# Graph attention on one core: the softmax issued in front of the other tiles' work, the finished rows made by VectorE in one operation

## The chip, the cores and the metric

One core of a Trainium2 chip runs the whole kernel. The metric is the device time of one execution in microseconds (us). Engines: PE is TensorE's matmul, PEld its weight load, DVE VectorE, ACT ScalarE, POOL GpSimd, SP SyncE, which here only issues DMAs.

## The reference, cut to what matters

Two layers follow one another: a graph attention on x (4 x 1024 rows of 512 features), then a transformer block (projections, attention, output projection, MLP) on its result. The change lies in the first. For each row and each of two directions d (the adjacency and its transpose), 16 heads attend to the first 20 rows of the same example:

```python
self_feat = concat(v, q) @ W_self.T + b_self
output = self_feat
for d in range(2):
    A = adj_f if d == 0 else swapaxes(adj_f, 1, 2)       # 11 labels
    A = A[:, :, :20, :]
    cond, vb = A.sum(-1), A @ w_bias + b_bias
    aff = einsum(q_d, k_d) / sqrt(32)
    aff = where(cond > 0, aff, -9e15) + vb
    w = softmax(aff)                                     # over 20
    output = output + (w @ kv) @ Wout_d + bout_d
return v + relu(output)
```

## The kernel before, in words

The program runs stage after stage, each a block of five instruction streams that ends with a barrier of all engines: `graph_tables`, `graph_attention`, `projections`, `attention`, `output_projection`, `mlp`. `graph_tables` folds the weights into tables, so that in `graph_attention` a tile of 128 rows needs one product for all logits (640 columns: 16 heads, 2 directions, 20 keys), one for the features (512 columns) and a small one that adds the attention's values onto the features in the same PSUM bank. Products are done as three products of split float32 (a high and a rest part).

`graph_attention` walks over 32 tiles, k = 0 to 31. Every engine has its own order, written out by hand, with semaphores between them:

- **TensorE**, in iteration k: in k = 18, 20, 22 and 24 four transposes of the next stage's rows (`z_transposes`, L615); `logits(k)` (L636 into `a_pa`, waits for `xl_done` and `lg_done`); `transposes(k + 1)` of x (L626, L627); `weights(k - 1)`, six transposes of the softmax (L668, waits for `p_done`); `features(k)` (L636 into `a_po`, two banks; waits until the rows of tile k - 2 are made from that bank, L658); `values(k - 1)` (L676, waits for `wt_copied`).
- **VectorE**, in `softmax(k)`: adds the bias to the logits (L769, twice), max (L777), subtraction of the max (L778, `sub_done`); the rest part of the next x (`x_rest`, L718); a flag column (`flag(k + 2)`, L713); `bias(k + 1)`: sum of the weighted adjacency (L725, waits for ScalarE's `prod_done`), count of labels (L726), mask (L727), their sum (L728); in k = 9, 11, ..., 23 the rest of an eighth of the next stage's weights (L790); in k = 10 to 24 the next stage's first rows (`first_rows`, L733 to L760); then, after Exp, the sum (L793), reciprocal (L794) and product (L795, `p_done`).
- **ScalarE**: rounds x out of PSUM (`x_rounded(k + 1)`, L541, L542), copies the transposed softmax (`weights_out(k - 1)`, L548 to L550), makes the row sum of x (`row_sum(k + 2)`, L560) and the eleven weighted adjacency planes (`weighted(k + 1)`, L569), then Exp (L599), then Relu of the rows (`rows_out(k - 1)`, L556), and on even k from 8 to 22 rounds an eighth of the next stage's weights (L605).
- **GpSimd** adds x to the rows after Relu (L524), frees the x buffer (`x_free`), and issues the store of y (L527); once, at k = 14, it makes the rstd of the first rows.
- **SP** loads x (four buffers, L490, waits for `x_free`) and the adjacency (two buffers, L492, waits for `adj_used`), at k = 5, 13 and 21 the next example's tables, at k = 6 the 4 MB of the next stage's weights (L504), at k = 8 the first four tiles of y.

The function `link` raises a semaphore when an operation is done and lets VectorE wait for it, so that the next operation reads finished data.

Of the kernel before, what the change touches and what calls it, by code (L numbers as in the profile page):

```python
# [14 lines left out]
ALU = mybir.AluOpType  # L15
# [377 lines left out]
def graph_attention(nc, t, ident, mod_t, gp, cg, pn, y, wqk, wqk_raw, x_first):  # L393
# [15 lines left out]
    with ExitStack() as ctx:  # L409
        def sb(name, shape, dt=F32):  # L410
# [26 lines left out]
        px = banks(ctx, nc, "a_px", 2)  # L437
        pw = banks(ctx, nc, "a_pw", 2)
        (st_in, ws_done, zeros_set, dve_step, rs_done, xt_done, xh_copied, xl_done, o_done, a_done, adj_used, lg_done,
         sub_done, exp_done, p_done, wt_done, wt_copied, pv_done, relu_done, y_done, x_free, w_in) = sems(  # L440
            ctx, nc, "graph", "st_in ws_done zeros_set dve_step rs_done xt_done xh_copied xl_done o_done a_done adj_used lg_done sub_done "
            "exp_done p_done wt_done wt_copied pv_done relu_done y_done x_free w_in", first=True)
        x_in = sems(ctx, nc, "graph", " ".join("x_in%d" % i for i in range(4)))
        wqk_in, wqk_rounded = sems(ctx, nc, "graph", "wqk_in wqk_rounded")
        (rows_in, half_set, stats_done, aggr_done, var_ready, rstd_ready, z_done, zt_done, xm_done, first_rounded, first_split) = sems(
# [6 lines left out]
        def x5s(k):  # L452
            return x5[k % 4]
# [55 lines left out]
        @block.gpsimd  # L509
        def _(pool):  # L510
            for k in range(2):
                pool.memset(c4[k][:].bitcast(F32), 0.0).then_inc(zeros_set, 1)
                pool.memset(bd[k][:], 0.0).then_inc(zeros_set, 1)
            for k in range(4):
                pool.memset(x5[k][:, F:], 0.0).then_inc(zeros_set, 1)
            pool.wait_ge(zeros_set, 8)
            for k in range(4):
                pool.memset(x5[k][:, F + 1:F + 4:2], 1.0).then_inc(zeros_set, 1)

            pool.memset(half[:], -0.5).then_inc(half_set, 1)  # L520
            pool.sem_inc(x_free, 4)
            for k in range(B * BT):
                pool.wait_ge(relu_done, k + 1)
                pool.tensor_tensor(yo[k % 2][:], yo[k % 2][:], x5s(k)[:, 0:F], ALU.add).then_inc(y_done, 1)  # L524
                pool.wait_ge(y_done, k + 1)
                pool.sem_inc(x_free, 1)
                pool.dma_start(y[k * P:(k + 1) * P, :], yo[k % 2][:]).then_inc(y_out[k % 2], 16)  # L527
                if k == LN0 + GT:
                    pool.wait_ge(half_set, 1)
                    pool.wait_ge(var_ready, 1)  # L530
                    pool.tensor_tensor(rstd[:], ve[:], half[:], ALU.pow).then_inc(rstd_ready, 1)
            for n in range(2):
                pool.wait_ge(y_out[n], 16 * B * BT // 2)

        @block.scalar
        def _(act):
            def x_rounded(k):
                act.wait_ge(xt_done, k + 1)
                if k >= 2:
                    act.wait_ge(o_done, k - 1)  # L540
                act.copy(xh[k % 2][:, 0:F], px[0][:])  # L541
                act.copy(xh[k % 2][:, F:], px[1][:, 0:P]).then_inc(xh_copied, 1)  # L542

            def weights_out(k):
                act.wait_ge(wt_done, k + 1)
                if k:
                    act.wait_ge(pv_done, k)
                act.copy(wt[:, 0:4, :], pw[0][0:HC * HJ, :].rearrange("p (c n) -> p c n", n=P))  # L548
                act.copy(wt[:, 4, :], pw[1][0:HC * HJ, 0:P])
                act.copy(wt[0:HJ, 5, :], pw[1][0:HJ, P:2 * P]).then_inc(wt_copied, 1)  # L550

            def rows_out(k):
                act.wait_ge(pv_done, k + 1)
                if k >= 2:
                    act.wait_ge(y_out[k % 2], 16 * (k // 2))
                act.activation(yo[k % 2][:], po[k % 2][:], ACT.Relu).then_inc(relu_done, 1)  # L556

            def row_sum(k):
                act.wait_ge(x_in[k % 4], 16 * (k // 4 + 1))
                act.activation(x_copy[:], x5s(k)[:, 0:F], ACT.Copy, accum_out=rs[:, k % 2:k % 2 + 1]).then_inc(sum_done, 1)  # L560

            def weighted(k):
                act.wait_ge(adj_in[k % 2], 16 * (k // 2 + 1))
                if k == 0:
                    act.wait_ge(w_in, 32)
                else:
                    act.wait_ge(prod_read, k)
                for l in range(L0):
                    i = act.activation(prod[:, l, :], adj[k % 2][:, l, :], ACT.Copy, scale=wrow[:, l:l + 1])  # L569
                i.then_inc(prod_done, 1)  # L570

            def modulate(n):
                act.wait_ge(zt_done, n + 1)
                if n:
                    act.wait_ge(first_split, n)
                for c in range(KC):
                    i = act.activation(xm[:, c, :], px[0][:, c * P:(c + 1) * P], ACT.Identity,
                                       bias=mod_t[:, 0, c:c + 1], scale=mod_t[:, 0, KC + c:KC + c + 1])
                i.then_inc(xm_done, 1)

            n = B * BT
            tables(act, 0)
            row_sum(0)
            x_rounded(0)
            row_sum(1)
            weighted(0)
            for k in range(n):
                if (k - Z0) % 2 == 0 and 0 < (k - Z0) // 2 <= GT:
                    modulate((k - Z0) // 2 - 1)
                if k + 1 < n:  # L590
                    x_rounded(k + 1)
                if k:
                    weights_out(k - 1)
                if k + 2 < n:
                    row_sum(k + 2)
                if k + 1 < n:
                    weighted(k + 1)
                act.wait_ge(sub_done, k + 1)
                act.activation(lg[k % 2][:], lg[k % 2][:], ACT.Exp).then_inc(exp_done, 1)  # L599
                if k:  # L600
                    rows_out(k - 1)
                w = (k - W0) // 2
                if (k - W0) % 2 == 0 and 0 <= w < len(WN):
                    act.wait_ge(wqk_in, 16)
                    act.copy(w_part(wqk[0], w), w_part(wqk_raw, w)).then_inc(wqk_rounded, 1)  # L605
            weights_out(n - 1)
            rows_out(n - 1)

        @block.tensor
        def _(pe):  # L610
# [43 lines left out]
            def features(k):  # L654
                if k == 0:
                    pe.wait_ge(ws_done, 2)
                if k >= 2:
                    pe.wait_ge(relu_done, k - 1)  # L658
                product(po[k % 2][:], (xh[k % 2], xl[k % 2]), (wsh, wsl), c4[(k // BT) % 2][:, 0:F]).then_inc(o_done, 1)

            def weights(k):
# [35 lines left out]
        def _(dve):  # L697
            steps = [0]

            def link(ins):  # L700

                steps[0] += 1
                ins.then_inc(dve_step, 1)
                dve.wait_ge(dve_step, steps[0])
# [4 lines left out]
            def flag(k):  # L709
                if k == 0:  # L710
# [2 lines left out]
                dve.tensor_scalar(x5s(k)[:, F:F + 3:2], rs[:, k % 2:k % 2 + 1].to_broadcast([P, 2]), 0.0, None,  # L713
                                  ALU.not_equal).then_inc(rs_done, 1)

            def x_rest(k):
                dve.wait_ge(xh_copied, k + 1)
                dve.tensor_tensor(xl[k % 2][:], px[0][:], xh[k % 2][:, 0:F], ALU.subtract).then_inc(xl_done, 1)  # L718

            def bias(k):  # L720

                s = sm[k % 2]
                dve.wait_ge(adj_in[k % 2], 16 * (k // 2 + 1))
                dve.wait_ge(prod_done, k + 1)
                dve.reduce_sum(s[:, 0, :], prod[:].rearrange("p l j -> p j l"), axis=AX.X).then_inc(prod_read, 1)  # L725
                link(dve.reduce_sum(s[:, 1, :], adj[k % 2][:].rearrange("p l j -> p j l"), axis=AX.X))  # L726
                link(dve.tensor_scalar(s[:, 2, :], s[:, 1, :], 0.0, NEG, ALU.is_le, ALU.mult))  # L727
                i = dve.scalar_tensor_tensor(out=s[:, 3, :], in0=s[:, 0, :], scalar=wrow[:, L0:L0 + 1], in1=s[:, 2, :],  # L728
                                             op0=ALU.add, op1=ALU.add)
                link(i)  # L730
                dve.sem_inc(adj_used, 1)
# [30 lines left out]
            def softmax(k):  # L762
# [17 lines left out]

                if k + 1 < B * BT:
                    x_rest(k + 1)
                if k + 2 < B * BT:
                    flag(k + 2)
                if k + 1 < B * BT:
                    bias(k + 1)
                w = (k - 1 - W0) // 2
                if (k - 1 - W0) % 2 == 0 and 0 <= w < len(WN):
                    dve.wait_ge(wqk_rounded, w + 1)
                    dve.tensor_tensor(w_part(wqk[1], w), w_part(wqk_raw, w), w_part(wqk[0], w), ALU.subtract)  # L790
                first_rows(k)
                dve.wait_ge(exp_done, k + 1)
                link(dve.reduce_sum(dn[:], z[:], axis=AX.X))  # L793
                link(dve.reciprocal(dn[:], dn[:]))  # L794
                dve.tensor_tensor(z[:], z[:], dn[:].unsqueeze(2).to_broadcast([P, 2 * H0, M0]),  # L795
                                  ALU.mult).then_inc(p_done, 1)

            n = B * BT
            flag(0)
# [1137 lines left out]
```

## Time and profile before

| | us |
|---|---|
| median of 3 runs | 3224.87 (3224.06 to 3225.6) |
| the profiled execution, its own time | 3222.87 |
| its span | 3221.1 |
| `graph_attention`, first transpose of x to last store's issue | 184.4 to 536.4 |

| engine | busy us | share of the span |
|---|---|---|
| PE | 3076.9 | 96% |
| PEld | 2440.8 | 76% |
| DVE | 1850.5 | 57% |
| ACT | 1341.9 | 42% |
| POOL | 845.7 | 26% |

Busy shares are means over stages with different limits. A row of the timeline gives the start of an instruction from the span's start, its duration, engine, line, operation, what it writes and reads with partitions and elements, how many were merged (x), and in brackets the idle time of its engine before it and what ended that.

### The profile page before, as it was taken

What the parts mean: (1) busy time and instruction counts of PE and PEld (TensorE: products, weight loads), DVE (VectorE), ACT (ScalarE), POOL (GpSimd) and SP (SyncE); (2) the same over time, 40 slices, a digit from 0 to 9 for tenths busy, and PEclk for the clock granted to TensorE, in tenths of its full rate; (3) what the DMA queues carried; (4) which work ended last, traced back from release to release, by engine and by line L of the source; (5) the groups of instructions that cost most, each with busy time, mean ns of one, the idle gap of its engine ahead of it and who ended that gap; (6) DMA issues with size and microseconds to landing.
All of it is one profiled execution on the core that took longest, in us unless ns stands there. A gap on an engine that the chain in (4) does not pass through costs nothing. (4 is left out here: it accounts for less than half of the span.)

```text
span 3221.1 us, 62151 instructions
## 1 busy us (share of the span) xinstructions
PE 3076.9 (96%) x24696; PEld 2440.8 (76%) x24696; DVE 1850.5 (57%) x2743; ACT 1341.9 (42%) x2786; POOL 845.7 (26%) x571
## 2 busy tenths in 40 slices
PE   8969998999999799999999999999896999999999
PEld 5968887888888577777777777777685888888887
DVE  4357785212211388888888888888564334333432
ACT  2145653222222277777777777777002111111111
POOL 1011112100000143444444344436454111111110
PEclk9989998999999899999999999999997999999999
DMA  4554222333332333233333333332563001010100
GB/s 140 178 183 145 96 70 97 107 106 104 104 114 102 105 110 96 80 94 92 94 80 93 92 94 81 92 97 70 215 241 111 1 27 33 26 33 26 33 14 14
DMA packets 196342, 297.28 MB, mean 92 GB/s; under 512 B 27889, under 2 KB 105713, under 8 KB 194055
## 3 DMA queue, kind: packets, MB, share of 16 engines
q1 hardware_dynamic: 182528, 276.54, 27.6%
q0 software_dynamic: 4288, 14.68, 1.3%
q10 hardware_dynamic: 9296, 2.77, 0.4%
q8 instruction: 172, 2.82, 0.4%
q14 instruction: 58, 0.47, 0.0%
HBM read 190.44 MB, written 103.49 MB: 91 GB/s over the span
## 5 line engine op out<-in xcount | busy, mean ns | idle before, releaser
L1338 DVE TENSOR_REDUCE b_nm<-b_ps 128x1 f32<-128x1024 f32 x512 | 601.6, 1216 | 16.3 <-PE b_ps L1279 3.2
L1245 ACT ACTIVATE b_p<-b_ps,b_nm 128x1024 f32<-128x1024 f32 x512 | 565.0, 1113 | 40.8 <-DVE b_nm L1338 40.8
L1308 PE MATMUL b_po<-b_pt,b_v 128*64 128x256 f32 x4096 | 498.3, 385 | 0.8 <-DVE b_pt L1358 0.8
L1250 ACT ACTIVATE b_pt<-b_tp_act 128x512 f32<-128x512 f32 x512 | 308.6, 603 | 305.1 <-PE b_tp_dve L1291 305.1
L1358 DVE COPY b_pt<-b_tp_dve 128x512 f32<-128x512 f32 x512 | 351.2, 686 | 117.3 <-PE b_tp_dve L1291 117.2
L1291 PEld LDWEIGHTS b_tp_act<-ident,b_p 64*128 64x128 f32 x4096 | 312.2, 138 | 128.8 <-issue 100.6
L1308 PEld LDWEIGHTS b_po<-b_pt,b_v 128*64 128x64 f32 x4096 | 271.9, 136 | 128.6 <-ACT b_pt L1250 0.9
L1291 PE MATMUL b_tp_act<-ident,b_p 64*128 64x64 f32 x4096 | 347.8, 225 | 2.4 <-issue 2.4
L1291 PE MATMUL b_tp_dve<-ident,b_p 64*128 64x64 f32 x4096 | 347.7, 225 | 0.0
L1700 ACT ACTIVATE d_ge<-d_pf,d_b 128x512 f32<-128x512 f32 x128 | 88.2, 689 | 596.6 <-PE d_pf L1722 596.6
L1291 PEld LDWEIGHTS b_tp_dve<-ident,b_p 64*128 64x128 f32 x4096 | 311.8, 138 | 2.4
L1789 DVE CAST d_gh<-d_ge 128x512 fp32r<-128x512 f32 x128 | 69.7, 544 | 417.8 <-ACT d_ge L1700 417.7
L1279 PE MATMUL b_ps<-b_kl,b_qh 64*128 64x512 f32 x1024 | 225.9, 435 | 18.4 <-DVE b_kl L1382 14.5
L1191 POOL TENSOR_TENSOR b_qh<-b_raw_q,b_ones 128x1024 fp32r<-128x1024 f32 x62 | 117.5, 1895 | 426.2 <-DMA b_raw_k<-k_t 400.7
L955 ACT ACTIVATE p_qk<-p_pm 128x512 f32<-128x512 f32 x128 | 76.6, 598 | 322.6 <-PE p_pm L977 322.6
L1733 PE MATMUL d_po<-d_w2h,d_gl 128*128 128x512 f32 x512 | 205.4, 401 | 2.0 <-DVE d_gl L1791 2.0
L1279 PE MATMUL b_ps<-b_kh,b_qh 64*128 64x512 f32 x1024 | 205.7, 393 | 0.0
L1279 PE MATMUL b_ps<-b_kh,b_ql 64*128 64x512 f32 x1024 | 204.4, 391 | 0.0
L1733 PE MATMUL d_po<-d_w2h,d_gh 128*128 128x512 f32 x512 | 202.5, 395 | 0.0
L1733 PE MATMUL d_po<-d_w_rest,d_gh 128*128 128x512 f32 x512 | 201.9, 394 | 0.0
L1660 POOL TENSOR_TENSOR d_y<-d_y,d_gated 128x512 f32<-128x512 f32 x32 | 43.2, 1374 | 559.7 <-DVE d_gated L1796 559.7
L1195 POOL TENSOR_TENSOR b_ql<-b_raw_q,b_qh 128x1024 fp32r<-128x1024 f32 x62 | 147.6, 2380 | 4.9
(253 smaller groups left out, 5666.8 us busy)
## 6 DMA issues: line engine op xcount, KB each, us to landing
b_raw_q<-q_t SPq DMA_DIRECT2D x128, 256.0 KB, 4.3
q_t<-p_qk SPq DMA_DIRECT2D x64, 256.0 KB, 2.0
k_t<-p_qk SPq DMA_DIRECT2D x64, 256.0 KB, 2.0
v_n<-p_vs SPq DMA_DIRECT2D x32, 512.0 KB, 3.2
b_raw_k<-k_t SPq DMA_DIRECT2D x128, 128.0 KB, 4.2
b_v<-v_n SPq DMA_DIRECT2D x32, 512.0 KB, 3.9
b_rb<-inv SPq DMA_DIRECT2D x64, 256.0 KB, 3.8
o_t<-b_ot SPq DMA_DIRECT2D x32, 512.0 KB, 2.6
```

What stands on the lines that cost most here:

```text
L955: act.activation(qk[n % 4][:], pm[n % 4][:], ACT.Copy, scale=float(D1) ** -0.5 if n < PAIRS else 1.0).then_inc(qk_done, 1)
L1191: pool.tensor_tensor(qh[u][h][:], raw_q[h][:], one, ALU.mult)
L1195: pool.tensor_tensor(ql[u][h][:], raw_q[h][:], qh[u][h][:], ALU.subtract)
L1245: act.activation(pr[k % 4][:], ps[k % 2][:], ACT.Exp, bias=nm[:, k % 4:k % 4 + 1], accum_out=rs[:, n:n + 1]).then_inc(exp_done, 1)
L1250: act.activation(dst, src, ACT.Copy).then_inc(t_out[0], 1)
L1279: mm = pe.matmul(ps[k % 2][:, half * SK:(half + 1) * SK], q[u][h][HALF[half], q0:q0 + P], key[u][h][HALF[half], :], start=(n == 0), stop=( ...
L1291: mm = pe.transpose(tp(j, k)[:, kc * D1:(kc + 1) * D1], pr[k % 4][HALF[j], kc * P:(kc + 1) * P], ident[HALF[j], HALF[j]])
L1308: mm = pe.matmul(po[rows, (blk % 2) * 2 * P:(blk % 2 + 1) * 2 * P], vt[u][:, kc, rows], pt[blk % 2][h][:, kc, :], start=(kc == 0), stop=(k ...
L1338: dve.tensor_reduce(nm[:, k % 4:k % 4 + 1], ps[k % 2][:], axis=AX.X, op=ALU.max, negate=True).then_inc(max_done, 1)
L1358: dve.tensor_copy(dst, src).then_inc(t_out[1], 1)
L1700: act.activation(ge[j % 2][:], pf[j % 2][:], ACT.Gelu, bias=b1[:, j:j + 1]).then_inc(gelu_done, 1)
L1733: mm = pe.matmul(po[n][:], a[j % 2][:, cols], w[:, j, :], start=(j == 0 and m == 0), stop=(j == NH - 1 and m == 2))
```

## The change

VectorE's softmax waits for Exp and does its sum, reciprocal and product right behind `x_rest(k + 1)`, in front of `flag(k + 2)`, `bias(k + 1)`, the next stage's weights and the first rows; ScalarE does Exp right behind `weights_out(k - 1)`, in front of the row sum and the weighted adjacency. In `bias`, the label count and the mask come in front of the wait for the weighted adjacency. The finished rows, max(rows, 0) + x, are made by one `scalar_tensor_tensor` of VectorE out of PSUM, behind `bias(k + 1)`; ScalarE's Relu and GpSimd's addition are gone, and the semaphore `relu_done` with them. GpSimd still frees the x buffer and issues the store.

```diff
@@ semaphores
-         sub_done, exp_done, p_done, wt_done, wt_copied, pv_done, relu_done, y_done, x_free, w_in) = sems(
+         sub_done, exp_done, p_done, wt_done, wt_copied, pv_done, y_done, x_free, w_in) = sems(
@@ gpsimd
             for k in range(B * BT):
-                pool.wait_ge(relu_done, k + 1)
-                pool.tensor_tensor(yo[k % 2][:], yo[k % 2][:], x5s(k)[:, 0:F], ALU.add).then_inc(y_done, 1)
                 pool.wait_ge(y_done, k + 1)
                 pool.sem_inc(x_free, 1)
@@ scalar
-            def rows_out(k):
-                act.wait_ge(pv_done, k + 1)
-                if k >= 2:
-                    act.wait_ge(y_out[k % 2], 16 * (k // 2))
-                act.activation(yo[k % 2][:], po[k % 2][:], ACT.Relu).then_inc(relu_done, 1)
...
                 if k:
                     weights_out(k - 1)
+                act.wait_ge(sub_done, k + 1)
+                act.activation(lg[k % 2][:], lg[k % 2][:], ACT.Exp).then_inc(exp_done, 1)
                 if k + 2 < n:
                     row_sum(k + 2)
                 if k + 1 < n:
                     weighted(k + 1)
-                act.wait_ge(sub_done, k + 1)
-                act.activation(lg[k % 2][:], lg[k % 2][:], ACT.Exp).then_inc(exp_done, 1)
-                if k:
-                    rows_out(k - 1)
...
             weights_out(n - 1)
-            rows_out(n - 1)
@@ tensor, features(k)
                 if k >= 2:
-                    pe.wait_ge(relu_done, k - 1)
+                    pe.wait_ge(y_done, k - 1)
@@ vector
+            def rows_out(k):
+                dve.wait_ge(pv_done, k + 1)
+                if k >= 2:
+                    dve.wait_ge(y_out[k % 2], 16 * (k // 2))
+                dve.scalar_tensor_tensor(out=yo[k % 2][:], in0=po[k % 2][:], scalar=0.0, in1=x5s(k)[:, 0:F],
+                                         op0=ALU.max, op1=ALU.add).then_inc(y_done, 1)
@@ vector, bias(k)
                 dve.wait_ge(adj_in[k % 2], 16 * (k // 2 + 1))
+                link(dve.reduce_sum(s[:, 1, :], adj[k % 2][:].rearrange("p l j -> p j l"), axis=AX.X))
+                dve.tensor_scalar(s[:, 2, :], s[:, 1, :], 0.0, NEG, ALU.is_le, ALU.mult)
                 dve.wait_ge(prod_done, k + 1)
-                dve.reduce_sum(s[:, 0, :], prod[:].rearrange("p l j -> p j l"), axis=AX.X).then_inc(prod_read, 1)
-                link(dve.reduce_sum(s[:, 1, :], adj[k % 2][:].rearrange("p l j -> p j l"), axis=AX.X))
-                link(dve.tensor_scalar(s[:, 2, :], s[:, 1, :], 0.0, NEG, ALU.is_le, ALU.mult))
+                link(dve.reduce_sum(s[:, 0, :], prod[:].rearrange("p l j -> p j l"), axis=AX.X))
+                dve.sem_inc(prod_read, 1)
@@ vector, softmax(k)
                 if k + 1 < B * BT:
                     x_rest(k + 1)
+                dve.wait_ge(exp_done, k + 1)
+                link(dve.reduce_sum(dn[:], z[:], axis=AX.X))
+                link(dve.reciprocal(dn[:], dn[:]))
+                dve.tensor_tensor(z[:], z[:], dn[:].unsqueeze(2).to_broadcast([P, 2 * H0, M0]),
+                                  ALU.mult).then_inc(p_done, 1)
                 if k + 2 < B * BT:
                     flag(k + 2)
                 if k + 1 < B * BT:
                     bias(k + 1)
+                if k:
+                    rows_out(k - 1)
...
                 first_rows(k)
-                dve.wait_ge(exp_done, k + 1)
-                link(dve.reduce_sum(dn[:], z[:], axis=AX.X))
-                link(dve.reciprocal(dn[:], dn[:]))
-                dve.tensor_tensor(z[:], z[:], dn[:].unsqueeze(2).to_broadcast([P, 2 * H0, M0]),
-                                  ALU.mult).then_inc(p_done, 1)
+                if k == B * BT - 1:
+                    rows_out(k)
```

## Rows read from the trace of the kernel before

**Rows 1.** Waits of TensorE's weight loads, 180 to 545 us: total, times, longest
```profile
PEld a_pw L668 <- DVE a_lg L795: 30.6, 32, 2.5
```

**Rows 2.** Timeline of a plain tile: TensorE and its weight loads around the logits' end
```profile
493.52 0.31 PE L636 MATMUL a_pa<-a_c,a_xh 128*128 128x320 f32 x1
...
494.44 0.59 PEld L668 LDWEIGHTS a_pw<-ident,a_lg 128*120 128x120 f32 x6 [0.30 <-DVE a_lg L795]
...
495.04 0.76 PEld L636 LDWEIGHTS a_po<-a_wsh,a_xh 128*128 128x128 f32 x4
```

**Rows 3.** Timeline of GpSimd: the additions of tiles 0, 26 and 30
```profile
210.96 1.29 POOL L524 TENSOR_TENSOR a_yo<-a_yo,a_x 128x512 f32<-128x512 f32 x1 [34.67 <-ACT a_yo L556]
...
490.54 1.29 POOL L524 TENSOR_TENSOR a_yo<-a_yo,a_x 128x512 f32<-128x512 f32 x1 [7.51 <-ACT a_yo L556]
...
530.35 1.25 POOL L524 TENSOR_TENSOR a_yo<-a_yo,a_x 128x512 f32<-128x512 f32 x1 [7.52 <-ACT a_yo L556]
```

**Rows 4.** Timeline of VectorE in the same plain tile
```profile
490.34 1.00 DVE L726 TENSOR_REDUCE a_sm<-a_adj 128x40 f32<-128x440 int32 x1
491.37 0.51 DVE L727 TENSOR_SCALAR a_sm<-a_sm 128x40 f32<-128x40 f32 x1
491.91 0.26 DVE L728 SCALAR_TENSOR_TENSOR a_sm<-a_sm,a_wrow 128x40 f32<-128x40 f32 x1
492.32 0.82 DVE L793 TENSOR_REDUCE a_dn<-a_lg 128x32 f32<-128x640 f32 x1
493.17 0.35 DVE L794 RECIPROCAL a_dn<-a_dn 128x32 f32<-128x32 f32 x1
493.56 0.82 DVE L795 TENSOR_TENSOR a_lg<-a_lg,a_dn 128x640 f32<-128x640 f32 x1
494.30 0.88 DVE L769 TENSOR_TENSOR a_lg<-a_pa,a_sm 128x320 f32<-128x320 f32 x2
495.33 0.82 DVE L777 TENSOR_REDUCE a_mx<-a_lg 128x32 f32<-128x640 f32 x1
496.18 0.83 DVE L778 TENSOR_TENSOR a_lg<-a_lg,a_mx 128x640 f32<-128x640 f32 x1
496.92 0.68 DVE L718 TENSOR_TENSOR a_xl<-a_px,a_xh 128x512 fp32r<-128x512 f32 x1
497.52 0.16 DVE L713 TENSOR_SCALAR a_x<-a_rs 128x2 f32<-128x2 f32 x1
499.38 1.00 DVE L725 TENSOR_REDUCE a_sm<-a_prod 128x40 f32<-128x440 f32 x1 [1.70 <-ACT a_prod L569]
```

**Rows 5.** Timeline of ScalarE in the same plain tile
```profile
496.14 0.64 ACT L560 ACTIVATE a_x_copy<-a_x 128x512 f32<-128x512 f32 x1
...
496.77 2.51 ACT L569 ACTIVATE a_prod<-a_adj,a_wrow 128x40 f32<-128x40 int32 x11
...
499.18 0.73 ACT L599 ACTIVATE a_lg<-a_lg 128x640 f32<-128x640 f32 x1
```

**Rows 6.** VectorE's groups, 208 to 520 us: count, busy us, mean ns, idle
```profile
L790 DVE TENSOR_TENSOR w_qk_rest<-w_qk_raw,w_qk_high 128x1024 fp32r<-128x1024 f32 x8 | 9.8, 1225 | 1.2
```

**Rows 7.** Timeline of ScalarE: the row sum that waited for its load of x
```profile
248.99 0.63 ACT L560 ACTIVATE a_x_copy<-a_x 128x512 f32<-128x512 f32 x1 [2.09 <-DMA a_x<-x]
```

**Rows 8.** Timeline of VectorE in the first tile, GpSimd idle
```profile
191.59 0.18 DVE L727 TENSOR_SCALAR a_sm<-a_sm 128x40 f32<-128x40 f32 x1
```

**Rows 9.** Timeline of TensorE's weight loads: one of the four z-transposes
```profile
424.84 0.42 PEld L615 LDWEIGHTS a_px<-ident,a_zn 128*128 128x128 f32 x4
```

**Rows 10.** Timeline of SP's queue in the plain tile
```profile
491.91 0.33 SPq L490 DMA_DIRECT2D a_x<-x  x1
```

**Rows 11.** Tile a_x, 180 to 540 us: the loads' time from issue to landing
```profile
DMA to landing us min/median/max: 2.6/2.7/6.4
```

**Rows 12.** Timeline of the stage's end: the last Relu and the last store's issue
```profile
533.82 0.60 ACT L556 ACTIVATE a_yo<-a_po 128x512 f32<-128x512 f32 x1 [2.23 <-PE a_po L676]
...
536.35 0.56 POOL L527 DMA_DIRECT2D y<-a_yo  x1 [0.59 <-POOL a_yo L524]
```

More of the change, by code:

```diff
@@ L439, in graph_attention @@
         (st_in, ws_done, zeros_set, dve_step, rs_done, xt_done, xh_copied, xl_done, o_done, a_done, adj_used, lg_done,
-         sub_done, exp_done, p_done, wt_done, wt_copied, pv_done, relu_done, y_done, x_free, w_in) = sems(
+         sub_done, exp_done, p_done, wt_done, wt_copied, pv_done, y_done, x_free, w_in) = sems(
             ctx, nc, "graph", "st_in ws_done zeros_set dve_step rs_done xt_done xh_copied xl_done o_done a_done adj_used lg_done sub_done "
-            "exp_done p_done wt_done wt_copied pv_done relu_done y_done x_free w_in", first=True)
+            "exp_done p_done wt_done wt_copied pv_done y_done x_free w_in", first=True)
         x_in = sems(ctx, nc, "graph", " ".join("x_in%d" % i for i in range(4)))
```

## The prediction

> **What bounds the kernel now.** The change stays inside the graph-attention stage, so I read the waits of that stage first. The row to see is TensorE's wait for the normalised softmax: the weight load of the transposes that turn the softmax (L668) waited for VectorE's last multiplication (L795) in each of the 32 tiles, 30.6 us in all [rows 1]; no other wait of TensorE comes back tile by tile. Then the timeline of one plain tile, with the end of its logits, 493.52 + 0.31 = 493.83, as zero. TensorE goes on with the transposes of the next tile, stops 0.30 us before L668, starts the features at 1.21 [rows 2], and is dense from there to the next logits. The last four turns are plain, (530.35 - 490.54) / 4 = 9.95 us by GpSimd's additions [rows 3], so a plain turn holds 9.65 us of TensorE's own work. The 30 turns between the first and the last full tile took 530.35 - 210.96 = 319.4 us, 10.65 each [rows 3]: 20.9 us above 30 plain turns.
>
> What makes the turn is a loop over three engines: VectorE's L795, TensorE's transposes L668, ScalarE's copies out of them, row sum and eleven weighted copies (L569), and back to VectorE, which idles 1.70 us for L569 at L725, then does the bias and only then the softmax's sum, reciprocal and product [rows 4, 5]. Everything else VectorE does behind the bias lengthens this loop in full: the eight rests of the next stage's weights at 1.23 us each (L790 [rows 6]) and the next stage's first rows. That is the 20.9, but for some 2.6 around one late load of x (ScalarE idled 2.09 us for it [rows 7]), which leaves 18.3 us in tiles 9 to 24.
>
> **The change, part by part.**
>
> *Softmax in front.* After the change the product of tile k hangs on logits(k) alone, through the adds, max, subtraction, Exp, sum, reciprocal and product. Start to start [rows 4, 5]: 1.03 + 0.85, then subtraction, Exp and two semaphore hops 0.83 + 0.73 + 0.10 = 1.66 (the rest of the next x, 0.68, fits inside), then 0.85 + 0.39 + 0.74: done 5.5 us after zero. TensorE wants it in front of the next L668, at 9.65 + 0.31 = 9.96. The 4.4 us between them are the cover; the 30.6 us go, all but the last tile's 0.3, which has nothing behind it: **-30.3 us**. ScalarE must reach Exp in time: the rounding of x and the three copies occupy it until about 2.3, the subtraction ends at 2.8. The row sum and weighted copies, 0.63 + 2.51 [rows 5], now follow Exp and end at 6.7; VectorE wants them at 6.9, so its 1.70 us of idleness goes too. The adjacency count is put ahead of that wait, and adds nothing; it is the cover of L569.
>
> *Finished rows on VectorE.* ScalarE loses 32 Relus, GpSimd 32 additions of 1.29 us [rows 3], neither on the path except at the end. VectorE gains 32 operations of 128x512 with one source in PSUM. No row shows this operation at this size. The nearest is L718, 128x512 out of PSUM with a second source in SBUF: 0.68 us, next start 0.60 later [rows 4]. That is the lower end and what I take. The upper end is one column at half that rate: L790 did 1024 columns in 1.23 us [rows 6], so 1.23. The same operation at 40 columns (L728) took 0.26 against 0.18 for L727 undisturbed [rows 4, 8], which does not exclude it. The Trainium skill speaks against the change here ("Vector Engine (DVE) Microarchitecture Reference", "7. Points that are easy to get wrong"): this operation halves its throughput when both sources are non-bf16 and in SBUF. One source here is in PSUM, so its condition is not met as written; no row decides it. By it the sum would be that of the first rival below.
>
> *GpSimd off VectorE's back.* L727 took 0.51 us while GpSimd's addition ran (490.54 to 491.83) and ended as that did; at 191.59, with GpSimd idle, 0.18 [rows 3, 4, 8]. The addition goes, so I count 0.18.
>
> *VectorE's new turn.* 1.03 + 0.85 + 1.66 + 0.85 + 0.39 + 0.74, flag 0.15, adjacency count 1.03, mask 0.18, sum of the weighted copies 1.00 with 0.15 for its semaphore and wait, L728 0.41, rows 0.60: **9.05 us**, against TensorE's 9.65. A plain tile is TensorE's, with 0.6 us to spare. That cover is gone in tiles 9 to 24: the 18.3 us of extra work less 16 x 0.6, less the four z-transposes of 0.42 by which TensorE's turn is longer there [rows 9], leaves 7.0 us of backlog. What is late next are the rows: features(k+1) overwrite the bank of tile k-1 and wait until its rows are made. These end at 9.2 after zero, features want them at 9.65 + 0.91 = 10.56, so 1.35 us of backlog are free. The rest is paid: **+5.6 us**.
>
> *The queues.* The rows' operation now gives x's buffer free, 9.2 after zero or 0.45 before the next, where GpSimd's addition did it at 491.83, 2.0 before [rows 3]. SP issues the load 0.08 us later [rows 10], which behind GpSimd's wake-up is at -0.3; it lands after 2.7 [rows 11], at 2.4, and ScalarE wants it at 3.5. In the stretch of the 4 MB load, x landed after 6.4 us [rows 11]. Then the loop rows, load, row sum, weighted copies, sum, L728, rows is 0.3 + 6.4 + 0.63 + 2.51 + 0.1 + 1.15 + 0.41 + 0.70 = 12.2 against 9.65; less the 1.35 free: **+1.2 us**. Before, that event's 2.1 us sat in the 30.6. GpSimd's queue keeps its store and only loses the addition; the store's buffer was filled two turns ago. VectorE's wait for the values of tile k-1 (done at about 6) stands in front of the rows (8.5), with nothing idle.
>
> *The end of the stage.* From Relu's start 533.82 to the last store's issue 536.35 were 2.53 us [rows 12]; now one operation 0.70 and the same 0.6 to the issue: **-1.2 us**. It is exposed, since the next stage loads y behind a barrier.
>
> Sum: -30.3 + 5.6 + 1.2 - 1.2 = -24.7 on the profiled 3222.87 us (span 3221.1), 3198.2. The median of the runs shown lies 2.0 us higher, so **3200 us**. No later stage changes.
>
> **Rivals.**
>
> *The rows' operation at half rate.* VectorE's turn becomes 9.6, the plain spare 0.05: backlog 18.3 - 0.8 - 1.7 - 1.35 = 14.5, and the load's 2.5 are never made good: 3222.9 - 31.5 + 14.5 + 2.5 + 2.0 = 3210. For it: two float32 sources and L728's 0.26. Against it: L718. Chance 0.12.
>
> *VectorE is quicker than its gaps say.* The semaphore gaps between linked operations, some 0.4 us, could vanish in work in flight. At 8.6 the spare is 16 x 1.05 = 16.8 beside the 1.7, and the 18.3 fit in; only the load's 1.2 is left: 3222.9 - 31.5 + 1.2 + 2.0 = 3194.6. For it: a few 0.15 us gaps in the row starts. Against: they were there before. Chance 0.10.
>
> *Exp comes late.* If ScalarE reaches Exp not at 2.3 but a microsecond behind the subtraction (the copies wait for L668, which waits behind the transposes), VectorE idles in each tile, its turn is 10.05, with the extra work 10.65 on average: 3224, no change. This is also how the change fails to do what it says, the wait for L795 being replaced by one for Exp. Against it: the 0.5 us margin. Chance 0.05.
>
> *The x load closes a loop (slower).* At SP's queue: the loop above is 5.8 us plus the landing. At 2.7 it is 8.5; it takes over from TensorE at 3.85, equals the old 10.65 at 4.85, and at 5.2 every turn is 11.0, over 30 turns +10 us: 3235. Before, the buffer came free 1.5 us earlier against the same zero. For it: 6.4 was seen once. Against it: the median 2.7. Chance 0.05.
>
> **How the numbers follow.** My forecast has 0.68, the rivals 0.12, 0.10, 0.05, 0.05. A measurement of this kernel tells about 0.2%, 6.4 us, from no change. The first three cases lie below 3218: faster 0.90, same 0.05, slower 0.05. The range takes in the quick and the half-rate case, 3193 to 3211; the last two are left out.
>
> **What would show it.** Right: the wait of L668 near zero; a plain turn of 9.65 at the ends of the stage; in tiles 13 to 24 a wait of the features (L636) for VectorE's rows, about 6 us in all; rows at 0.7 us; L727 at 0.18; no wait of VectorE for L569; last store issued about 27 us earlier than 536. Wrong: rows of 1.2 us, a wait of the sum for Exp over 0.2 us a tile, or ScalarE waiting for x in plain tiles.

## The result: 3201.3 us, 0.74% faster

| | median us | runs | ratio to the kernel before, 95% interval |
|---|---|---|---|
| before | 3224.86 | 3224.06 to 3225.60 | |
| changed | 3201.26 | 3199.87 to 3203.45 | 0.9926 (0.9914 to 0.9939) |

The forecast was 3200, with 3193 to 3211 as its range. The profiled execution of the changed kernel is its slowest, 3203.45 us, so its trace shows more waiting than a typical run; `changed_again` below is a second trace of the same kernel. In the changed kernel's lines L766 is the adds, L774 the max, L775 the subtraction, L714 the rest of x, L781 to L783 sum, reciprocal and product, L702 the flag, L720 and L721 count and mask, L723 the sum of the weighted copies, L725 the last bias operation, L709 the finished rows, L657 the softmax's transposes, L625 the products.

The page of the changed kernel, its first two lines:

```profile
span 3201.7 us, 62119 instructions
PE 3076.4 (96%) x24696; PEld 2442.9 (76%) x24696; DVE 1861.2 (58%) x2775; ACT 1326.0 (41%) x2754; POOL 803.6 (25%) x539
```

TensorE's busy time is what it was (3076.9). VectorE gained 11 us, ScalarE lost 16, GpSimd 42; the span lost 19.4. A busy share says nothing of this: what went was TensorE's waiting. The waits of TensorE's weight loads in the stage, 180 to 545 us (total, times, longest):

```profile
PEld a_po L625 <- DVE a_yo L709: 7.2, 10, 2.4
PEld a_po L665 <- ACT a_wt L548: 1.3, 1, 1.3
PEld a_px L615 <- ACT a_xm L569: 1.1, 3, 0.4
PEld a_pw L657 <- DVE a_lg L783: 0.7, 1, 0.7
```

The wait for the softmax's product, 30.6 us in 32 tiles [rows 1], is one of 0.7 us in the last tile. What came in its place stands above it: the features wait for the finished rows in 10 tiles, 7.2 us. The weight loads of the features that waited, from the timeline:

```profile
255.82 0.76 PEld L625 LDWEIGHTS a_po<-a_wsh,a_xh 128*128 128x128 f32 x4 [2.36 <-DVE a_yo L709]
285.73 0.77 PEld L625 LDWEIGHTS a_po<-a_wsh,a_xh 128*128 128x128 f32 x4 [0.83 <-DVE a_yo L709]
325.19 0.76 PEld L625 LDWEIGHTS a_po<-a_wsh,a_xh 128*128 128x128 f32 x4 [0.71 <-DVE a_yo L709]
...
457.10 0.76 PEld L625 LDWEIGHTS a_po<-a_wsh,a_xh 128*128 128x128 f32 x4 [0.34 <-DVE a_yo L709]
```

The first, 2.4 us, is the late load of x. The other nine, 4.9 us, lie between 285 and 457 us. VectorE's other work (the weights' rests, the next stage's first rows) begins only at 294.5, so the wait at 285.73 is not backlog. It follows a second late load of x: one issued at 274.53 held ScalarE until 280.19, 5.7 us later, and VectorE idled for ScalarE's copies:

```profile
280.19 0.63 ACT L552 ACTIVATE a_x_copy<-a_x 128x512 f32<-128x512 f32 x1 [2.34 <-DMA a_x<-x]
```

```profile
283.35 1.00 DVE L723 TENSOR_REDUCE a_sm<-a_prod 128x40 f32<-128x440 f32 x1 [1.12 <-ACT a_prod L561]
```

Up to 380 us ScalarE waited for x four times more, 1.7 us in all. In the second trace it waits for no x after 250 us, and the features wait 2.3 us there instead of 4.9. So in this trace backlog and late loads are mixed; what delayed these later loads is open.

VectorE's timeline in a tile at the end of that stretch and the start of the next:

```profile
465.88 0.88 DVE L766 TENSOR_TENSOR a_lg<-a_pa,a_sm 128x320 f32<-128x320 f32 x2
466.91 0.82 DVE L774 TENSOR_REDUCE a_mx<-a_lg 128x32 f32<-128x640 f32 x1
467.76 0.83 DVE L775 TENSOR_TENSOR a_lg<-a_lg,a_mx 128x640 f32<-128x640 f32 x1
468.51 0.69 DVE L714 TENSOR_TENSOR a_xl<-a_px,a_xh 128x512 fp32r<-128x512 f32 x1
...
469.40 0.82 DVE L781 TENSOR_REDUCE a_dn<-a_lg 128x32 f32<-128x640 f32 x1 [0.20 <-ACT a_lg L587]
470.25 0.35 DVE L782 RECIPROCAL a_dn<-a_dn 128x32 f32<-128x32 f32 x1
470.64 0.83 DVE L783 TENSOR_TENSOR a_lg<-a_lg,a_dn 128x640 f32<-128x640 f32 x1
471.38 0.16 DVE L702 TENSOR_SCALAR a_x<-a_rs 128x2 f32<-128x2 f32 x1
471.45 0.99 DVE L720 TENSOR_REDUCE a_sm<-a_adj 128x40 f32<-128x440 int32 x1
472.48 0.18 DVE L721 TENSOR_SCALAR a_sm<-a_sm 128x40 f32<-128x40 f32 x1
472.58 0.99 DVE L723 TENSOR_REDUCE a_sm<-a_prod 128x40 f32<-128x440 f32 x1
473.72 0.26 DVE L725 SCALAR_TENSOR_TENSOR a_sm<-a_sm,a_wrow 128x40 f32<-128x40 f32 x1
474.21 0.69 DVE L709 SCALAR_TENSOR_TENSOR a_yo<-a_po,a_x 128x512 f32<-128x512 f32 x1 [0.23 <-DVE a_sm L725]
...
475.55 0.89 DVE L766 TENSOR_TENSOR a_lg<-a_pa,a_sm 128x320 f32<-128x320 f32 x2 [0.65 <-PE a_pa L625]
```

The product starts 4.8 us behind the adds. From 465.88 to 475.55 the turn is 9.67, TensorE's, and VectorE idles the last 0.65 of it. While it still catches up its turn is its own, to be read off SP's issues of x, which follow the rows: 466.05 to 474.98 is 8.93, then 474.98 to 484.63 is 9.65.

```profile
466.05 0.33 SPq L490 DMA_DIRECT2D a_x<-x  x1
...
474.98 0.33 SPq L490 DMA_DIRECT2D a_x<-x  x1
...
484.63 0.33 SPq L490 DMA_DIRECT2D a_x<-x  x1
```

The stage's end, last rows and last store, from VectorE's and GpSimd's timelines:

```profile
513.80 0.69 DVE L709 SCALAR_TENSOR_TENSOR a_yo<-a_po,a_x 128x512 f32<-128x512 f32 x1 [3.04 <-PE a_po L665]
...
515.09 0.54 POOL L525 DMA_DIRECT2D y<-a_yo  x1 [3.19 <-DVE a_yo L709]
```

The last store is issued 21.3 us earlier than the 536.35 of before [rows 12], and 1.29 us behind the start of the last rows instead of 2.53.

### The profile page after: what moved, and what is told of

Its sections match the earlier page's. It is cut to its first block and busy times, and to the rows that moved or that the text cites. A ratio compares the mean times of both kernels' runs of the same rounds, so it can differ in the third digit from the quotient of the medians.

```text
span 3201.7 us, 62119 instructions
## 1 busy us (share of the span) xinstructions
PE 3076.4 (96%) x24696; PEld 2442.9 (76%) x24696; DVE 1861.2 (58%) x2775; ACT 1326.0 (41%) x2754; POOL 803.6 (25%) x539
## 5 line engine op out<-in xcount | busy, mean ns | idle before, releaser
L1280 PE MATMUL b_ps<-b_kl,b_qh 64*128 64x512 f32 x1024 | 226.1, 436 | 18.3 <-DVE b_kl L1383 14.7
```

The costliest lines, as they stand in the source:

```text
L1280: mm = pe.matmul(ps[k % 2][:, half * SK:(half + 1) * SK], q[u][h][HALF[half], q0:q0 + P], key[u][h][HALF[half], :], start=(n == 0), stop=( ...
```

## The experiments

The ratios are to the kernel before as it was measured beside each version, 3224.1 to 3224.4 us. The diffs show the main places of each edit.

The theory going in: the softmax in front brings the whole gain; the rows on VectorE give some of it back, as backlog where VectorE has other work; TensorE's turn of 9.67 us is the floor. The rivals differ by experiment and stand in the expectations.

**The softmax alone.** The kernel before with only the softmax's and the bias' new order.

```diff
@@ gpsimd, against the changed kernel
+                pool.wait_ge(relu_done, k + 1)
+                pool.tensor_tensor(yo[k % 2][:], yo[k % 2][:], x5s(k)[:, 0:F], ALU.add).then_inc(y_done, 1)
...
@@ scalar, against the changed kernel
                 if k + 1 < n:
                     weighted(k + 1)
+                if k:
+                    rows_out(k - 1)
@@ vector, against the changed kernel
                     bias(k + 1)
-                if k:
-                    rows_out(k - 1)
```

> Only the softmax is moved to the front (with the bias' new order); Relu stays on ScalarE, the addition on GpSimd. Theory (the softmax in front brings all of the gain, and VectorE's added row operation gives some of it back as backlog in tiles 9 to 24): TensorE's wait for L795 falls from 30.6 us to under 1; VectorE's turn is some 0.5 us shorter than with the rows (8.4 against 8.9), so the 7.2 us that the features wait for rows in the changed kernel fall to about 0.5, and the stage's end costs 1.2 us more: about 3196 us, 29 below the kernel before. Rival (the rows on VectorE bring a part of the gain of their own, by freeing ScalarE and GpSimd): 3205 to 3215 us.

Measured: 3195.77 us (3194.57 to 3196.29), ratio to the kernel before 0.9911 (0.9896 to 0.9926). The waits of TensorE's weight loads:

```profile
PEld a_pw L668 <- DVE a_lg L787: 0.7, 1, 0.7
PEld a_pa L636 <- DVE a_xl L718: 0.6, 2, 0.3
```

No wait for rows is among them, and the theory's 3196 is met. So half of the change is faster than the whole, by 5.5 us of 3201.3. The late load of x is here too (issued at 241.20, ScalarE waits 3.39 us for it until 249.19), but TensorE loses only one of these 0.3 us to it: with the rows off VectorE a late x is nearly free.

**The rows alone.** The kernel before with only the rows moved.

```diff
                 if k + 1 < B * BT:
                     bias(k + 1)
+                if k:
+                    rows_out(k - 1)          # VectorE, scalar_tensor_tensor out of PSUM
...
                 first_rows(k)
                 dve.wait_ge(exp_done, k + 1)
```

> Only the rows are moved to VectorE; the softmax's second half stays behind the other work. Theory (the loop VectorE, TensorE, ScalarE, VectorE sets the turn, and the rows lie in it): each turn grows by the rows' 0.8 us less the 0.3 us that L727 no longer loses to GpSimd, 32 x 0.5 = 16, less 1.2 at the stage's end: about 3240 us. Rival (either half brings part of the gain): 3210 to 3220 us.

Measured: 3239.88 us (3237.27 to 3241.08), ratio 1.0047 (1.0033 to 1.0061): slower than before, as the theory had it. The old wait grew from 30.6 us, because the rows lie in the loop that leads to the product:

```profile
PEld a_pw L663 <- DVE a_lg L799: 40.0, 30, 3.9
```

That the time came out at the expected 3240 is partly luck. A plain turn is 10.28 us (L663 at 495.54 and 505.82), 0.33 more than before and not the 0.5 that the theory counts. The stage is 14.6 us longer, and the waits explain only 9.4 of them. Most of the rest is TensorE's granted clock. Three times it is at 0.50, the level of 1.2 GHz: from 260.0 to 263.0, from 349.0 to 352.0 and from 407.0 to 410.0 us, each time shortly behind a wait of TensorE (3.9, 2.3 and 2.2 us). Its mean is 0.89 over 255 to 270, 0.91 over 340 to 360 and 0.89 over 400 to 416, which is 1.6, 1.8 and 1.8 us of full clock, 5.2 together. The first of these stretches, with its granted clock behind the engines' busy times:

```profile
255.00:270.00 15.00, 11.36 (x64) 10.02 (x63) 11.97 (x22) 5.32 (x19) 1.08 (x2) 0.89 0.42 127
```

The kernel before never leaves 1.00 between 200 and 500 us, although its longest wait there is 2.5 us; and a wait of 2.4 us at 325.82 of this run was followed by no fall. What decides is not shown.

The parts don't add: -28.4 and +15.7 make -12.7 where both together make -23.6. Behind the softmax the rows lie in VectorE's spare time; in front of it they lie on the path.

**The bias' old order.** The changed kernel, with the adjacency count behind the wait for ScalarE's weighted copies again.

```diff
-                link(dve.reduce_sum(s[:, 1, :], ...adj...))
-                dve.tensor_scalar(s[:, 2, :], ...)
                 dve.wait_ge(prod_done, k + 1)
-                link(dve.reduce_sum(s[:, 0, :], ...prod...))
-                dve.sem_inc(prod_read, 1)
+                dve.reduce_sum(s[:, 0, :], ...prod...).then_inc(prod_read, 1)
+                link(dve.reduce_sum(s[:, 1, :], ...adj...))
+                link(dve.tensor_scalar(s[:, 2, :], ...))
```

> The changed kernel with the bias' own order as it was: the sum of the weighted copies first, then count and mask. Theory (the adjacency count is the cover of ScalarE's weighted copies): VectorE idles 1.0 us a tile for L569's copies, its turn goes from 8.93 to 9.9 us, so it and not TensorE sets the turn of 9.9 in plain tiles, and the 18.3 us of other work in tiles 9 to 24 are paid in full: about 3217 us. Rival (VectorE's spare 0.7 us takes it up, only the tiles 9 to 24 lose): 3205 us.

Measured: 3225.06 us (3222.10 to 3228.56), ratio 1.0003 (0.9994 to 1.0012): the whole gain is gone. Its waits, and VectorE's idle time for the copies in a plain tile:

```profile
DVE a_sm L721 <- ACT a_prod L561: 37.6, 32, 2.3
PEld a_po L625 <- DVE a_yo L709: 27.6, 27, 3.1
```

```profile
494.14 1.00 DVE L721 TENSOR_REDUCE a_sm<-a_prod 128x40 f32<-128x440 f32 x1 [0.95 <-ACT a_prod L561]
```

The mechanism is the theory's (0.95 us idle a tile where 1.0 was expected), the sum was not: 3217. VectorE's turn here is 9.85 us (x issued at 487.70, 497.56, 507.40), 0.10 less than the old plain turn, and on it come the same 18.3 us of other work and a late load, as before the change. That is the old time less a few us, and I had taken off some 8 too many. Of these 8, 1.6 are the granted clock: 0.50 from 261.5 to 264.0 us, behind a wait of 3.1 us for rows, a mean of 0.89 over 255 to 270. So the order of two small operations carries as much as the order of the softmax, once the rows lie on VectorE. This run does not say what it is worth without them.

**The rows at double cost.** The changed kernel with a second such operation in tiles 0 to 30, into a scratch tile; the output is unchanged.

```diff
+                if k < B * BT - 1:
+                    dve.scalar_tensor_tensor(out=extra[:], in0=po[k % 2][:], scalar=0.0, in1=x5s(k)[:, 0:F], ...)
                 dve.scalar_tensor_tensor(out=yo[k % 2][:], in0=po[k % 2][:], ...).then_inc(y_done, 1)
```

> The changed kernel with the rows' operation preceded in tiles 0 to 30 by a copy of itself into a scratch tile (no effect on the output): the price that a halved rate would have had. Theory (VectorE has 0.7 us to spare in a plain turn and none in tiles 9 to 24): the plain turn stays 9.67 us, 0.6 us in each of tiles 9 to 24 is paid in full and the free margin falls from 1.35 to 0.75: +9 to +10 us, about 3211 us. Rival (TensorE is the bound all through and the rows are hidden): within 2 us of the changed kernel.

Measured: 3215.09 us (3213.46 to 3216.30), ratio 0.9971 (0.9960 to 0.9982): 13.8 us above the changed kernel, not 9 to 10. The waits, and two of the features' loads ahead of the busy stretch:

```profile
PEld a_po L626 <- DVE a_yo L713: 18.9, 20, 2.9
```

```profile
223.56 0.77 PEld L626 LDWEIGHTS a_po<-a_wsh,a_xh 128*128 128x128 f32 x4 [0.64 <-DVE a_yo L713]
...
244.32 0.76 PEld L626 LDWEIGHTS a_po<-a_wsh,a_xh 128*128 128x128 f32 x4 [1.43 <-DVE a_yo L713]
```

VectorE's turn is 9.54 (its adds at 497.32 and 506.86). With 0.13 to spare it hardly works off what delays it, so TensorE waits in the first tiles already and enters the busy stretch with no free margin. The waits shown, 0.64 and 1.43 us, come 6 us behind the moments at which ScalarE had waited for x (217.50, 1.13 us; 238.18, 1.75 us): late loads again. Between the traces, the waits for rows grew by 11.7 us and those for the rest of x by 0.5; the granted clock, 0.50 from 258.0 to 261.0 us behind a wait of 2.9 us (mean 0.91 over 250 to 268), adds 1.6. The rival (rows hidden) is out; the theory's mechanism holds, with the first tiles and the clock left out of its sum.

**Both sources in SBUF.** One more operation of this kind in tiles 26 to 29, output unchanged.

```diff
+                if 26 <= k < 30:
+                    dve.scalar_tensor_tensor(out=extra[:], in0=stage[:, 0, :], scalar=0.0, in1=x5s(k)[:, 0:F], ...)
```

> The changed kernel with one more operation of the rows' kind in tiles 26 to 29, both float32 sources in SBUF, into a scratch tile (no effect on the output). If two float32 sources in SBUF halve the throughput, it takes 1.2 us; if the rate is that of the rows out of PSUM (0.69 us), 0.7. At 0.7 the plain turn stays 9.67 us in these tiles; at 1.2 the four tiles together run up 4 x 0.5 us of backlog, within the margin of 1.35 but for about 0.6 us.

Measured: 3199.78 us, one run. The operation by its tile (min, median, max ns), beside the rows of the changed kernel:

```profile
L711 DVE SCALAR_TENSOR_TENSOR a_extra<-a_stage,a_x x4: 691/692/693, 471.0 to 499.9; 128x512 f32<-128x512 f32 x4
```

```profile
L709 DVE SCALAR_TENSOR_TENSOR a_yo<-a_po,a_x x32: 685/692/693, 213.2 to 513.8; 128x512 f32<-128x512 f32 x32
```

0.69 us either way, no more than the subtraction of the same size (L714, 0.68). The rule cited in the prediction (the Trainium skill, "Vector Engine (DVE) Microarchitecture Reference", "7. Points that are easy to get wrong": half throughput with two non-bf16 sources in SBUF) is not what the chip does in this form of the operation, with float32 and without an accumulator; the measurement decides.

**The weights' rests on GpSimd.** The changed kernel; eight subtractions of 128x1024 leave VectorE's busy stretch.

```diff
                 pool.dma_start(y[k * P:(k + 1) * P, :], yo[k % 2][:]).then_inc(y_out[k % 2], 16)
+                w = (k - W0) // 2
+                if (k - W0) % 2 == 0 and 0 <= w < len(WN):
+                    pool.wait_ge(wqk_rounded, w + 1)
+                    pool.tensor_tensor(w_part(wqk[1], w), w_part(wqk_raw, w), w_part(wqk[0], w), ALU.subtract)
```

> The changed kernel, with the eight rests of the next stage's weights (9.7 us of VectorE in tiles 9 to 23) made by GpSimd, which has nothing else to do then. Theory (VectorE's backlog is what the features wait for): the 4.8 us of waits for rows in tiles 9 to 24 go, the 2.4 us at the late load of x stay: about 3196.5 us, 5 below the changed kernel. Rival (GpSimd's operation of some 2.4 us holds up VectorE's operations with two SBUF sources by what it spares them): 3201 us.

Measured: 3202.50 us (3201.59 to 3204.94), ratio 0.9934 (0.9921 to 0.9948): no gain, the rival's case. VectorE's group of the subtraction in the changed kernel, then in this one (count, busy us, mean ns, idle):

```profile
L775 DVE TENSOR_TENSOR a_lg<-a_lg,a_mx 128x640 f32<-128x640 f32 x30 | 24.8, 826 | 1.0
```

```profile
L779 DVE TENSOR_TENSOR a_lg<-a_lg,a_mx 128x640 f32<-128x640 f32 x30 | 35.9, 1195 | 1.0
```

11.1 us more in eight tiles, 1.39 each, where 1.22 each was taken off. The timeline of one:

```profile
293.15 2.41 POOL L529 TENSOR_TENSOR w_qk_rest<-w_qk_raw,w_qk_high 128x1024 fp32r<-128x1024 f32 x1
...
293.71 0.82 DVE L778 TENSOR_REDUCE a_mx<-a_lg 128x32 f32<-128x640 f32 x1
294.56 1.69 DVE L779 TENSOR_TENSOR a_lg<-a_lg,a_mx 128x640 f32<-128x640 f32 x1
```

The subtraction, both sources in SBUF, takes 1.69 us here instead of 0.83, up to 2.47 in other tiles, and Exp waits for it. In all eight it ends 0.7 us behind the end of GpSimd's operation (here 296.25 against 295.56), whenever it began: it makes little or no headway beside it. The max just before it, with one source, ran beside GpSimd at its usual 0.82. The rest of x begins only when GpSimd is done, so its 0.68 says nothing on this. The Trainium skill ("SBUF — State Buffer", "Who interferes with whom") has a two-source operation in SBUF contend with GpSimd's reads; the trace agrees.

**The load in four.** The changed kernel, the 4 MB of the next stage's weights in four loads.

```diff
-                    if k == W0 - 2:
-                        sp.dma_start(wqk_raw[:], ...[:, :, 0:2 * INNER]).then_inc(wqk_in, 16)
+                    if W0 - 2 <= k < W0 - 2 + KC:
+                        c = k - W0 + 2
+                        sp.dma_start(wqk_raw[:, c, :], ...[:, c, 0:2 * INNER]).then_inc(wqk_in, 16)
```

> The changed kernel, with the 4 MB load of the next stage's weights issued as four loads of 1 MB in four successive tiles. Theory (that load is what makes one x land after 8 us, and this costs 2.4 us of features' waits): the longest landing of x falls under 5 us, the 2.4 us go, the 4.8 us of backlog stay: about 3199 us. Rival (the late x comes from the tables' loads just before, or the cost only moves to other tiles): 3201 us, a landing of x still over 6 us.

Measured: 3197.04 us (3196.44 to 3197.70), ratio 0.9915 (0.9902 to 0.9929): 4.2 us below the changed kernel (3.5 below `changed_again`, whose runs lie above all of these), more than the 2.4 expected. The features' waits, and ScalarE's longest wait for x in the changed kernel and here:

```profile
PEld a_po L626 <- DVE a_yo L710: 2.6, 6, 0.7
```

```profile
250.32 0.63 ACT L552 ACTIVATE a_x_copy<-a_x 128x512 f32<-128x512 f32 x1 [3.92 <-DMA a_x<-x]
```

```profile
239.85 0.63 ACT L553 ACTIVATE a_x_copy<-a_x 128x512 f32<-128x512 f32 x1 [2.21 <-DMA a_x<-x]
```

The load of x behind the 4 MB landed after 8.0 us. Those issued among the four loads (245.40, 254.32, 264.00) landed after 2.7, 4.1 and 2.7. The wait shown last is for one issued just ahead of the first of the four, behind the tables' loads:

```profile
233.88 0.36 SPq L490 DMA_DIRECT2D a_x<-x  x1
```

It held ScalarE until 239.85, 6.0 us, so "under 5 us" was missed, and the tables' loads, which the rival names, may have their part. The longest landing that the profile lists, 5.0 us, is of a load at 331.97 that has nothing to do with the four; in the two traces of the changed kernel the same load took 5.2.

The features' waits fell from 7.2 to 2.6 us: from 2.4 to 0.7 at the late load, from 3.4 to 0.5 between 260 and 400 us, where this trace has no late x, and not behind 400 (1.5 and 1.4). Against the second trace of the changed kernel, with 4.3, it is 1.7. That the load in four is faster the runs show; how much of the 3.5 to 4.2 us is the load itself one pair of traces does not.

**Both on top of each.** `rows_on_vector_best` is the changed kernel with GpSimd's help and the load in four; `softmax_best` is the softmax alone with both; `softmax_and_load` is the softmax alone with the load in four only. `changed_again` is the changed kernel once more.

> The changed kernel with both: weights' rests on GpSimd and the load in four. Theory (backlog and load are two separate terms): both go, 3201.3 - 4.8 - 2.4 = 3194 us, the features' wait for rows under 0.5 us. Rival (they overlap or the gains don't add): 3197 us.

> The softmax in front alone (Relu on ScalarE, addition on GpSimd), with weights' rests on GpSimd and the load in four. Theory (TensorE's 9.67 us a turn is the floor, whoever makes the rows): like the version with the rows on VectorE but for 1.2 us at the stage's end: 3195 us. Rival (GpSimd with an addition of 1.3 and a rest of 2.4 us a tile holds VectorE up): 3198 us or more.

> The softmax in front alone (Relu on ScalarE, addition on GpSimd), with the 4 MB load in four; the weights' rests stay on VectorE. Theory (in the version with the softmax alone TensorE already waits for nothing that comes back, so neither the load nor GpSimd's help can give much): 3194 us, within 2 us of both the softmax alone (3195.8) and the version with GpSimd's help (3193.8). Rival (GpSimd's help is worth something once rows are off VectorE): 3196 us, level with the softmax alone.

> The changed kernel once more, beside the two others on the same chip: 3201 us; the features wait 7 us for rows, 2.4 of it at the late load of x.

| version | median us | runs | ratio, 95% interval |
|---|---|---|---|
| rows_on_vector_best | 3199.12 | 3198.81 to 3201.81 | 0.9925 (0.9911 to 0.9938) |
| softmax_best | 3193.84 | 3192.86 to 3195.25 | 0.9905 (0.9890 to 0.9921) |
| softmax_and_load | 3194.61 | 3193.72 to 3196.52 | 0.9906 (0.9891 to 0.9922) |
| changed_again | 3200.54 | 3198.47 to 3204.44 | 0.9927 (0.9914 to 0.9941) |

`rows_on_vector_best` was expected at 3194 (theory) or 3197 (rival) and came out above both: with rows on VectorE the two don't add, and GpSimd's help costs 2 us against the load in four alone. `changed_again` has the expected time, but its features wait 4.3 us for rows where 7 were expected: 2.0 at the late load, 0.9 between 260 and 400, 1.4 behind. With the softmax alone nothing more is to be had beyond 2 us, since TensorE waits for nothing that comes back. The three versions with the softmax alone overlap in their runs, so their order stays open; all three lie below every run of the changed kernel.

## Why the prediction was right, step by step

*What bounds.* The loop through the product was the bound: with the product in front the wait went from 30.6 to 0.7 us, and the softmax alone gives 28.4 us where the forecast's term was 30.3. In the traces the stage is 29.3 us shorter (184.4 to 536.4 against 184.7 to 507.4). Of the missing 1.0 us, 0.4 is the last tile's wait (0.7 where 0.3 was left), 0.3 a second short wait for the rest of x, the rest open; the other 0.9 of the time lies behind the stage, where the two traces of the changed kernel differ as much (0.9). TensorE's own plain turn is 9.67, forecast 9.65.

*VectorE's turn.* 8.93 us against 9.05. The rows' operation took 0.69, the value taken; L727's 0.51 fell to 0.18 as L721; the wait of the sum for Exp is 0.20 a tile, its start lying 1.64 behind the subtraction's against 1.66. VectorE's idle time for the copies went from 54 us to 5.2 in the stage.

*Backlog.* Forecast +5.6; measured about 2. The first trace has 4.9 us of such waits, but most of the 3.4 us before 400 goes with late loads of x; without those it is 0.9 or 0.5. Where no x is late behind the 4 MB, the waits are 2.3 us (second trace, 4.3 less the load's 2.0) and 1.9 (the load in four). The mechanism is right, its size was not: the turn was 0.12 quicker over 16 tiles, 2 us less backlog, and TensorE's 1.1 us of waits for ScalarE (see the end, below) gave VectorE as much time to catch up; this last is argued, not tested. In time the rows on VectorE cost 5.5 us net against the softmax alone, and the forecast's terms make 5.6 + 1.2 - 1.2 = 5.6. That these agree is partly luck: too much backlog stood in for late loads of which the sum had one.

*The load.* Forecast +1.2, measured 2.4 and 2.0. The step that was mis-sized is the landing: 6.4 us was taken from the trace of before, the changed kernel's two traces have 8.0 and 7.2. In place of 6.4 these give 2.8 and 2.0. The 4 MB load itself is issued at nearly the same time in all three (233.5 to 233.9); the load of x behind it comes at 242.3 instead of 242.6. The other late loads of the first trace were not in the forecast.

*The end.* 1.29 us for 2.53, forecast 1.3. The sign "about 27 us earlier than 536" does not follow from the forecast's own sum of 24.7; measured are 21.3, and 25 in the second trace (511.3). Not foreseen were 1.1 us in which the transposes wait for the next stage's first rows on ScalarE.

*Rivals.* The half rate did not occur (0.69 us); its price, 3210, was itself too low, as the doubled operation gave 3215 (1.6 of it the clock). Exp was not late (0.20 us). The x load closed the loop in single turns, not in all: at the 4 MB load and again at 280.19, where the load took 5.7 us and the turn from rows to rows (L709 at 273.76 and 284.98) 11.2. That one lies in front of VectorE's other work, so "ScalarE waiting for x in plain tiles", which the prediction names as a sign of being wrong, did occur once at that size. The quick case went too far: the turn of 8.93 lies between its 8.6 and the forecast's 9.05, nearer the latter, and the gaps it let vanish are there (0.23 ahead of L709, 0.20 for Exp).

## What to carry to other kernels

When a bottleneck engine waits for a product of another engine once a tile, look at what that engine does ahead of it that nobody waits for, and put it behind; what was exposed work becomes cover. Then count the full turn of the engine that got the work, its idle gaps included, against the turn of the bottleneck: half of this change is faster than all of it, since GpSimd and ScalarE had time for the rows and VectorE, in half of the tiles, had none. A buffer that comes free later is part of that price: the late load of x behind the 4 MB cost TensorE 0.3 us in the softmax alone and 2.0 to 2.4 in the changed kernel. An operation that needs no late input belongs in front of the wait for that input, however small: here the count of the adjacency, 1.0 us a tile, decided between all of the gain and none with the rows on VectorE. And add up the waits before you call a slower version explained: in the rows alone a third of the loss was no wait but TensorE's clock, which had fallen behind a few longer ones.

## What the runs showed of the hardware that was not expected

A `scalar_tensor_tensor` of 128x512 float32 takes 0.69 us with one source in PSUM and 0.69 with both in SBUF. A VectorE subtraction of 128x640 with both sources in SBUF took 1.69 to 2.47 us instead of 0.83 beside GpSimd's 2.4 us operation on other tiles, and ended 0.7 us behind it in all eight tiles: moving 1.22 us of work to GpSimd cost VectorE 1.39. Behind a 4 MB load a load of 256 KB landed after 8.0 us, where the median is 2.7; among four loads of 1 MB it took 2.7 to 4.1. TensorE's granted clock fell to 0.50 (1.2 GHz) behind waits of 2.2 to 3.9 us inside a busy stage and cost some 1.7 us each time; other waits of 2.4 and 2.5 us had no such fall.
